# Last stage of a transformer block: GpSimd adds expert rows of three groups, and two z loads move into the expert loop

## The reference

```
other = x[:, 1:]; h = gelu(other @ W1 + x[:, :1] @ W2 + b)           # 16 x 255 rows of 256
h = h + attention(layernorm(h))                                      # 16 heads of 64
z = layernorm(h)
routed = sum over the top 2 of 8 experts e of  prob_e * (silu(z @ w1[e]) @ w2[e])
shared = sigmoid(z @ gate_w) * ((silu(z @ G) * (z @ U)) @ down)
out = h + routed + shared
```

## Time and profile before

| | |
|---|---|
| median of 3 runs | 1081.71 us (1078.3 to 1083.3) |
| the profiled execution | 1082.13 us, span 1080.4 us |
| mean granted TensorE clock | 0.989 of full speed |
| busy | PE 94%, DVE 69%, ACT 61%, POOL 47% |
| expert loop | about 880 to 1033 us |
| first load of expert rows issued | 1036.3 us |
| last store issued | 1076.4 us |

### The profile page before, as it was taken

The page is one execution under the profiler, slowest core; times in us unless marked ns, Lnnn a source line. Parts: engine busy times, 40 slices in busy tenths (PEclk is TensorE's granted clock), DMA queues, the critical chain, the costliest instruction groups (busy, mean ns, idle before and its releaser), DMA issues.

```text
span 1080.4 us, 23154 instructions
## 1 busy us (share of the span) xinstructions
PE 1014.5 (94%) x8042; PEld 877.6 (81%) x8042; DVE 744.6 (69%) x1912; ACT 661.4 (61%) x1939; POOL 512.6 (47%) x557
## 2 busy tenths in 40 slices
PE   6979999999999999999999999999998899999995
PEld 6867889778887887888787788879786779999985
DVE  3757775776677577767757885775784566666667
ACT  4647774676577477747747784765685445555541
POOL 0016543557356455735554664555435387454430
PEclk9989999999999999999999999999999999999998
DMA  8110000001000000100000010000003643444479
GB/s 272 60 45 2 1 2 1 21 2 40 21 1 22 21 21 1 41 21 1 21 22 21 1 41 21 2 11 31 21 2 127 224 120 110 135 141 130 134 219 312
DMA packets 47496, 65.91 MB, mean 61 GB/s; under 512 B 7992, under 2 KB 39480, under 8 KB 47384
## 3 DMA queue, kind: packets, MB, share of 16 engines
q1 hardware_dynamic: 40056, 44.50, 13.2%
q0 software_dynamic: 7056, 19.93, 5.4%
q10 hardware_dynamic: 272, 0.00, 0.0%
HBM read 36.09 MB, written 28.33 MB: 60 GB/s over the span
## 4 chain that ended last, share of the span: by engine, by line
PE 69%; DVE 10%; ACT 6%; DMA 4%; issue 3%; SPq 2%; POOL 0%; DVEq 0%; ACTq 0%; POOLq 0%
PE proj_ps L70 11%; PE proj_ps L72 11%; PE proj_ps L71 11%; PE proj_ps L738 9%; PE pT_ps L725 9%; PE s_ps L711 8%; DMA back<-expert_out_rows 2%; ACT prob L1041 2%; PE s_ps L70 2%; PE s_ps L71 2%; PE s_ps L72 2%; PE s_ps L963 1%; PE pT_ps L984 1%; DVE probT L1288 1%; DVE z L1389 1%
## 5 line engine op out<-in xcount | busy, mean ns | idle before, releaser
L1041 ACT ACTIVATE prob<-s_ps,nmax 128x255 f32<-128x255 f32 x512 | 238.0, 480 | 154.7 <-DVE nmax L1263 154.6
L1716 POOL TENSOR_SCALAR prob<-prob,rinv 128x255 f32<-128x255 f32 x128 | 138.4, 1081 | 282.3 <-DVE rinv L1281 281.8
L1263 DVE TENSOR_REDUCE nmax<-s_ps 128x2 f32<-128x510 f32 x256 | 157.7, 678 | 7.6 <-PE s_ps L711 7.0
L725 PEld LDWEIGHTS pT_ps<-ident,prob 128*128 128x128 f32 x1024 | 114.6, 140 | 37.1 <-issue 28.5
L725 PE MATMUL pT_ps<-ident,prob 128*128 128x128 f32 x1024 | 137.0, 276 | 3.4 <-ACT probT L1067 3.0
L738 PE MATMUL proj_ps<-probT,v 128*64 128x256 f32 x1024 | 125.7, 387 | 1.5 <-DVE probT L1288 1.3
L1270 DVE TENSOR_TENSOR qk_space<-proj_ps,qk_space 128x512 fp32r<-128x512 f32 x128 | 88.2, 689 | 47.2 <-ACT qk_space L1053 45.2
L1718 POOL TENSOR_SCALAR prob<-prob,rinv 128x255 f32<-128x255 f32 x128 | 119.5, 934 | 0.0
L711 PE MATMUL s_ps<-qk_space 64*128 64x256 f32 x1536 | 109.1, 289 | 0.9 <-DVE qk_space L1270 0.9
L1048 ACT ACTIVATE prob<-prob,rinv 128x255 f32<-128x255 f32 x128 | 66.7, 521 | 70.5 <-DVE rinv L1281 70.4
L1041 ACT ACTIVATION_READ_ACCUMULATOR prob<-s_ps,nmax 128x1 f32 x512 | 108.9, 213 | 0.0
(11 more groups left out here) (257 smaller groups left out, 2701.9 us busy)
## 6 DMA issues: line engine op xcount, KB each, us to landing
xg<-expert_in_rows SPq DMA_DIRECT2D x71, 130.0 KB, 2.2
back<-expert_out_rows SPq DMA_DIRECT2D x6, 1024.0 KB, 21.2
xin<-in_x_dram SPq DMA_DIRECT2D x8, 512.0 KB, 4.9
z_rows<-z SPq DMA_DIRECT2D x8, 512.0 KB, 3.1
z<-z_rows SPq DMA_DIRECT2D x8, 512.0 KB, 4.2
expert_in_rows<-bo_row SPq DMA_DIRECT2D x16, 128.0 KB
raw_up<-in_L_ffn_w_dram SPq DMA_DIRECT2D x8, 256.0 KB, 5.5
raw_down<-in_L_ffn_w_dram SPq DMA_DIRECT2D x8, 256.0 KB, 6.7
```

The costliest lines, as they stand in the source:

```text
L725: m = pe.transpose(pT_ps[h][:, o:o + P], prob[u_par(u)][:, h, qt, kt * P:(kt + 1) * P], ident[:])
L1041: m = act.activation(prob[u_par(u)][:, h, qt, 1:N], s_ps[b][h][:, qt * N + 1:(qt + 1) * N], ACT.Exp, bias=nmax[b][:, n:n + 1], accum_out=r ...
L1263: dve.tensor_reduce(nmax[b][:, 2 * h:2 * h + 2], s_ps[b][h][:].rearrange("p (q k) -> p q k", q=2)[:, :, 1:N], AX_X, ALU.max, negate=True). ...
L1716: pool.tensor_scalar(prob[k][:, 0, 1, 1:N], prob[k][:, 0, 1, 1:N], rinv[k][:, 1:2], None, ALU.mult).then_inc(s_nA1, 1)
```

## The change

- The accumulating transfers are gone. Groups 0, 1 and 2 are loaded like the others, and POOL adds them to `resid` with two tensor-tensor instructions each (`ADDED_BY_POOL` = 3), counted on a semaphore of its own. DVE no longer has `add_experts(2)`.
- SP loads `back` in the order 0, 3, 1, 2, 4, 5, 6, 7. The stores of groups 0 to 2 wait for POOL's adds, the others for DVE's, in the old order.
- z of groups 6 and 7 get buffers of their own, over `prob2` and `z2`, which are dead then, and SP loads them in the expert loop right behind the load of tile 6 (`BUFS` = 6). The loads behind the loop are gone. `z3_at(g)` names the buffer, and the two loads share one semaphore, for which PE waits in full.

```diff
--- before.py
+++ after.py
@@ -456,7 +456,7 @@
         raw_gu = over("raw_gu", qkv_at, half, [DC, 2 * F])
         sd_hi, sd_lo = (over(n, qkv_at, part + k * FC * D, [FC, D], F32R) for k, n in enumerate(("sd_hi", "sd_lo")))
         raw_sd = over("raw_sd", qkv_at, part + FC * D, [FC, D])
-        z3 = [z, over("z3", qkv_at, part + half, [GT, D])]
+        z3 = [z, over("z3", qkv_at, part + half, [GT, D]), over("z3_6", at["prob2"], 0, [GT, D]), over("z3_7", at["z2"], 0, [GT, D])]
         z3T_hi = [over("z3T_hi0", qkv_at, 2 * part, [DC, GR], F32R), over("z3T_hi1", qkv_at, 4 * part + half, [DC, GR], F32R)]
         z3T_lo = [over("z3T_lo0", qkv_at, 2 * part + half, [DC, GR], F32R), over("z3T_lo1", at["probT1"], 0, [DC, GR], F32R)]
         h_hi, h_lo = ([over(n + "0", qkv_at, 3 * part + k * half, [FC, GR], F32R), other]
@@ -509,7 +509,7 @@
         s_wo, s_woe = sem("out_rows_in_psum"), sem("out_rows_added")
 
         s_gu_in, s_gu_hi, s_gu_w = sem("shared_in"), sem("shared_hi"), sem("shared_split")
-        s_z3_in = [sem(f"z3_in{k}") for k in range(2)]
+        s_z3_in = [sem(n) for n in ("z3_in0", "z3_in1", "z3_last_two_in")]
         s_zt3, s_zh3, s_zl3 = sem("z3T_in_psum"), sem("z3T_hi_ready"), sem("z3T_lo_ready")
         s_gu, s_silu, s_prod = sem("hidden_in_psum"), sem("silu_ready"), sem("gated_ready")
         s_hhi, s_hlo = sem("h_hi_ready"), sem("h_lo_ready")
@@ -526,10 +526,17 @@
         s_at = sem("y_at_ready")
         s_back = [sem(f"back{g}_in") for g in range(GROUPS)]
         s_first, s_gate = sem("first_added"), sem("gates_ready")
+        s_pool = sem("rows_added_by_pool")
         s_all, s_out = sem("rows_complete"), sem("out_stored")
 
         EXPERTS_FIRST = 7
-        ADDED_BY_DMA = 2
+        Z3_RING = 6
+
+        def z3_at(g):
+
+            return g % 2 if g < Z3_RING else g - Z3_RING + 2
+
+        ADDED_BY_POOL = 3
 
 
         FREE_P = 6
@@ -582,9 +589,9 @@
             def load_z3(g):
                 if g == 0:
                     sp.wait_ge(s_zt, DC * GROUPS)
-                elif g >= 2:
+                elif 2 <= g < Z3_RING:
                     sp.wait_ge(s_zt3, DC * (g - 1))
-                sp.dma_start(z3[g % 2][:], z_dram[g]).then_inc(s_z3_in[g % 2], 16)
+                sp.dma_start(z3[z3_at(g)][:], z_dram[g]).then_inc(s_z3_in[min(z3_at(g), 2)], 16)
 
             def load_expert(e):
                 sp.dma_start(raw_up[:, :, e, :], w1[e].rearrange("(c p) f -> p c f", p=P)).then_inc(s_raw[e], 16)
@@ -602,10 +609,10 @@
                              ).then_inc(s_back[g], 16)
 
             def store_group(g):
-                if g < ADDED_BY_DMA:
-                    sp.wait_ge(s_back[g], 16 * TOP)
+                if g < ADDED_BY_POOL:
+                    sp.wait_ge(s_pool, TOP * g + TOP)
                 else:
-                    sp.wait_ge(s_all, g + 1 - ADDED_BY_DMA)
+                    sp.wait_ge(s_all, g + 1 - ADDED_BY_POOL)
                 sp.wait_ge(s_added, 2 * g + 2)
                 rows = resid[:, GT * g:GT * g + GT, :].rearrange("p (b h) d -> p b h d", h=2)
                 sp.dma_start(out[2 * g:2 * g + 2, HEAD - 1:P - 1, :].rearrange("b p d -> p b d"),
@@ -645,15 +652,15 @@
 
             for n in range(RUN):
                 load_x(n)
-
-
-            load_z3(SHARED_EARLY + 2)
+                if n == BUFS:
+                    sp.wait_ge(s_o, ROUNDS * GROUPS)
+                    for g in range(Z3_RING, GROUPS):
+                        load_z3(g)
+
+
             for k in range(SLOTS):
                 sp.wait_ge(s_yst[k], 16 * len(range(k, RUN, SLOTS)))
-            for g in range(ADDED_BY_DMA, 4):
-                load_back(g)
-            load_z3(SHARED_EARLY + 3)
-            for g in range(4, GROUPS):
+            for g in (0, ADDED_BY_POOL, *range(1, ADDED_BY_POOL), *range(ADDED_BY_POOL + 1, GROUPS)):
                 load_back(g)
             for g in range(GROUPS):
                 store_group(g)
@@ -866,7 +873,7 @@
                     output_rows(g, 1, True)
 
             def transpose_z3(g):
-                pe.wait_ge(s_z3_in[g % 2], 16 * (g // 2 + 1))
+                pe.wait_ge(s_z3_in[min(z3_at(g), 2)], 16 * (g // 2 + 1 if g < Z3_RING else 2))
                 for c in range(DC):
                     if g == 0:
                         pe.wait_ge(s_exp, 2 * UNITS * GROUPS)
@@ -877,7 +884,7 @@
                         if g == 2:
                             pe.wait_ge(s_rank_read, GROUPS)
                     for t in range(GT):
-                        m = pe.transpose(z_ps[c][:, t * P:(t + 1) * P], z3[g % 2][:, t, c * P:(c + 1) * P], ident[:])
+                        m = pe.transpose(z_ps[c][:, t * P:(t + 1) * P], z3[z3_at(g)][:, t, c * P:(c + 1) * P], ident[:])
                     m.then_inc(s_zt3, 1)
 
             def hidden_part(g, c2, k):
@@ -1460,7 +1467,7 @@
             def add_shared(g):
                 dve.wait_ge(s_gate, 2 * g + 2)
                 if g >= EXPERTS_FIRST:
-                    dve.wait_ge(s_all, g + 1 - ADDED_BY_DMA)
+                    dve.wait_ge(s_all, g + 1 - ADDED_BY_POOL)
                 else:
                     dve.wait_ge(s_woe, 2 * g + 2 + FREE_W)
                 for j in range(2):
@@ -1644,7 +1651,7 @@
                 else:
                     dve.wait_ge(s_woe, 2 * g + 2 + FREE_W)
                 dve.tensor_tensor(rows, rows, back[g][:, 1], ALU.add).then_inc(s_first, 1)
-                dve.wait_ge(s_first, g + 1 - ADDED_BY_DMA)
+                dve.wait_ge(s_first, g + 1 - ADDED_BY_POOL)
                 dve.tensor_tensor(rows, rows, back[g][:, 0], ALU.add).then_inc(s_all, 1)
 
 
@@ -1654,7 +1661,6 @@
             product(4, 1)
             hidden_split_lo(4, 1)
             product(5, 0)
-            add_experts(2)
             hidden_split_lo(5, 0)
             z3_lo(6)
             product(5, 1)
@@ -1811,20 +1817,17 @@
             for n in range(RUN):
                 scatter(n)
 
-            def add_experts(g, k):
-                if k:
-                    pool.wait_ge(s_back[g], 16)
-                else:
-                    pool.wait_ge(s_added, 2 * g + 2)
-                rows = y_rows[ROWS * k + GR * g:ROWS * k + GR * (g + 1), :].rearrange("(p t) d -> p (t d)", t=GT)
-                pool.dma_start(resid[:, GT * g:GT * g + GT, :].rearrange("p t d -> p (t d)"), rows,
-                               accum_op=ALU.add).then_inc(s_back[g], 16)
-
-            for k in range(SLOTS):
-                pool.wait_ge(s_yst[k], 16 * len(range(k, RUN, SLOTS)))
-            for k in range(TOP):
-                for g in range(ADDED_BY_DMA):
-                    add_experts(g, k)
+            def add_experts(g):
+                rows = resid[:, GT * g:GT * g + GT, :]
+                pool.wait_ge(s_back[g], 16)
+                pool.wait_ge(s_added, 2 * g + 2)
+                pool.tensor_tensor(rows, rows, back[g][:, 1], ALU.add).then_inc(s_pool, 1)
+                pool.wait_ge(s_pool, TOP * g + 1)
+                pool.tensor_tensor(rows, rows, back[g][:, 0], ALU.add).then_inc(s_pool, 1)
+
+            for g in range(ADDED_BY_POOL):
+                add_experts(g)
+
 
 
 def u_par(u):
```

## The result

| | before | after |
|---|---|---|
| median | 1081.57 us (1078.3 to 1083.64, 13 runs) | 1086.32 us (1082.97 to 1089.7, 13 runs) |
| profiled execution | 1082.13 us, span 1080.4 | 1089.12 us, span 1087.4 |
| ratio to before | | 1.0047, 95% interval 1.0032 to 1.0062 |

The changed kernel is 0.5% slower. The forecast was 1082.9, with 1087.5 for its rival R1 (VectorE and GpSimd take exclusive turns at SBUF), and the traces show R1. The profiled execution of after is 2.8 us above its median, so its sum is larger than the median's.

The account below looks back on a forecast made before the run. PE, busy 94%, was taken as the bound, with DVE alone at the end of the last stage. Sum: 1082.13 - 1.0 - 0.4 + 1.6 + 1.0 = 1083.3, less 0.42: 1082.9 us; range 1077.5 to 1088.5.

Parts of the forecast that it names:

- R1: Rival, last stage: DVE's two-input instructions and POOL's adds take exclusive turns at SBUF, +6.2 instead of +1.6, 1087.5 us; chance 0.26.
- both signs: Forecast wrong if the last stage is shorter than 42 us or longer than 46, or the expert loop moves over 2 us.
- (a): Last stage: DVE loses `add_experts(2)` and a wait, 3.4 us, but PE bounds it, so `product(7,0)` starts 1.0 us earlier.
- R3: Rival, last stage: DVE's 3.4 us count in full because PE is no bound, 1077.9 us; chance 0.08.
- (b): Last stage, transfers: six loads replacing accumulating transfers cost nothing, and the 1.01 us wait for group 4 goes.
- (c): Last stage: POOL's six adds take 2.4 us each; SP, free earlier, issues the last stores faster, -0.4 us.
- (d): Last stage: POOL's adds slow DVE instructions reading two SBUF tensors, +1.6 us after idle time, bounds 0 to 6.2.
- The upper end: Last stage: each two-input DVE instruction waits until the POOL add under way has ended, `product(7,0)` 6.2 us later.
- the doubled 23% of `normalise_rows`: DVE beside POOL: four `normalise_rows` took 1.71 us against 1.39, 23% more; doubled to 2.6 us for the last stage.
- two rows: Evidence against turns: `normalise_rows` beside POOL only 1.71 us, and four tiny adds 0.77 us beside POOL and alone.
- (e): Expert loop: z loads of groups 6 and 7 delay tile 7, PE waits about +1.0 us, bounds 0 to 2.6.
- R2: Rival, last stage and loop: no POOL interference with DVE and no stall at tile 7, 1080.3 us; chance 0.16.

Follow-up runs that it names:

- e3: The changed kernel without GpSimd's six adds, the expert rows of groups 0 to 2 left out of the sum: 1082.27 us, ratio 0.9998.
- e1: The changed kernel with only POOL's part: z of groups 6 and 7 loaded where it was before the change: 1085.17 us, ratio 1.0025.

## Why the prediction came out as it did

The class and the range were right, the range because it was drawn to take in R1, which had a chance of 0.26. The likeliest case was not the one that happened, and by both signs that the prediction gave for itself it was wrong: the last stage took 49.1 us (45.4 and 3.7), where 46 was the limit, and the expert loop moved by 2.4, where 2 was. By the steps:

- **(a) DVE without `add_experts(2)`, PE the bound: right.** Predicted -1.0 us at `product(7,0)`. In e3 that is 1060.95 with the first load of rows at 1037.01, so 23.9 behind it; before 25.1: -1.15. The 1.01 us wait for group 4 is gone too. R3, in which DVE's 3.4 us count in full, is refuted by it.
- **(b), (c) Loads and POOL: right in kind.** No DVE add waits for its rows, POOL's adds took 2.4 us each where nothing held them. POOL began at 1043.33, 5.0 us behind the first issue (predicted 5.3). The tail was undersized: -1.3 or -1.4 measured in after, e1 and e3, -0.4 taken. I priced the issue of the last stores (1.3 us, 1.2 predicted) and not their landing: the very last lands 3.6 us after its issue in before and 2.4 in after, and in the tail 0.97 MB still move in before and 0.52 in after. One slip did no harm: at 301 GB/s group 4 would have come at 1055.6, which is 0.4 after DVE wants it.
- **(d) POOL beside DVE: the step that failed.** It was the term of the sum that was mis-sized: +1.6 taken, +7.4 measured (31.4 less 23.9 at `product(7,0)`). The upper end, worked out in turns, was 6.2 (its own terms, 0.3 + 2.3 + 2.4 + 2.4 less 1.0, give 6.4). The traces show turns: 8.6 us of waiting in four instructions, less 0.9 of idle time (0.61 and 0.32 in e3) is 7.7. In the medians it is less, 4 to 5 us (1086.32 against 1082.27 of e3, or 1.0047 against 0.9998 in the ratios). I took the doubled 23% of `normalise_rows` because two rows contradicted the turns. The first was no fair witness: `normalise_rows` reads one tensor, the rule quoted there is about two, so its 1.71 says nothing against it; and no run here sets a one-input instruction of DVE beside such an add. The second stays unexplained: the tiny adds read two SBUF tensors of 8 elements a partition, POOL's TENSOR_SCALAR beside them (0.93 us from 421.76) reads SBUF, and nothing is drawn out. What I should have seen is that rows of 8 elements are far from splits of 512 and adds of 1024, which left the upper end open and no reason to stay near the lower.
- **(e) z loads in the loop: right in kind, too small.** +1.0 taken, bounds 0 to 2.6 (by its own terms 902.0 + 0.3 - 900.02, so 2.3). PE waits 1.46 us for tile 7 in after and up to 1.98 in the other kernels. Over all 71 tiles the six kernels with these loads and six buffers need 140.0 to 140.5 us, the two without them 137.8 (before) and 138.5 (e1): +1.5 to +2.7, single executions each. The cost lies at the first tiles: up to the 11th `y_copy` the six need 20.8 to 22.5 us and the two 19.1, and from there to the last 117.7 to 119.4 against 118.7 and 119.3. So later tiles don't pay again; the wait at tile 7 was too small in the sum.
- **R2** (no interference, no stall at tile 7) is refuted by (d) and (e). **R1** is confirmed as a mechanism, at +7.4 in the profiled execution instead of +6.2, and its 1087.5 stands against 1086.3.

That the errors of (c) and (e), 0.9 too slow and 1.4 too fast, nearly cancel is luck: without (d) the sum gives 1081.3, and e3 measured 1082.27 at a ratio of 0.9998.

The sum for the profiled pair: -0.4 (start) + 2.4 (loop) - 1.1 + 7.4 (DVE stage) - 1.3 (tail) = +7.0, which is 1087.4 less 1080.4.

## What to carry to other kernels

Before giving GpSimd a long SBUF-to-SBUF operation to relieve VectorE, list VectorE's instructions with two SBUF inputs in that stretch: here each could wait for a whole GpSimd instruction, so an idle engine was not free capacity. Look for the wait inside the durations, not between the instructions, and if the work must go there, cut it short or use stretches in which VectorE reads PSUM. Loads put into a stream whose tiles come just in time stalled it here, and one buffer more removed that stall and pauses that had been there before. The buffer alone was worth more (0.55%, interval 0.36 to 0.74) than all else in this change.

## What the runs showed of the hardware

- POOL reading SBUF and DVE reading two SBUF tensors exclude each other for whole instructions, in both directions (DVE 0.69 to 2.93 and 1.22 to 3.42 us, POOL 2.4 to 3.21). POOL writing only (memset, 1.81 us) doesn't hold DVE; reading one input (copy, 1.90 us) does. DVE instructions with an input in PSUM kept their times (0.67, 1.27 for two). Against it stands one row that no run explains: adds of 8 elements beside a POOL instruction that reads SBUF, 0.77 us for four with it and without it.
- The granted clock of TensorE in after was 0.50, the lower of its two levels (1.2 and 2.4 GHz), from 1059.6 to 1065.0, and 1.00 again from 1067.0; PE had stood idle from 1056.6 on. DVE was busy 13.33 of 13.40 us from 1059.6 to 1073.0, so it cost nothing here. In e3 the clock is 1.00 from 1056 to 1070, with PE busy 6.00 of the 6.00 us ahead of that.
